# Cross-attention, MLP and normalised cross-attention on one core: the norm weights folded into the next matrices, three-product values and projection, the last two inverse head norms on VectorE

## The reference

```python
# layer 0 (a and b in the kernel)
q = layernorm(x, ln1_w, ln1_b) @ Wq            # 16 heads of 16
k, v = split(layernorm(ctx, ln2_w, ln2_b) @ Wkv)
x = x + softmax(q k^T / 4) v @ Wproj + bproj
x = x + gelu(layernorm(x, ln3_w, ln3_b) @ W1 + b1) @ W2 + b2
# layer 1 (c in the kernel)
q = rotate(rmsnorm(x) * norm_w @ wq);  k, v = split(ctx @ wkv);  k = rotate(k)
q, k = q / |q|, k / |k|                        # per head
x = x + softmax(4 q k^T) v @ wout
```

## Time and profile before

| | us |
|---|---|
| median of 3 runs | 366.83 |
| the three runs | 367.35, 366.83, 364.96 |
| the profiled execution, whole | 367.27 |
| its span, first to last instruction | 365.5 |
| PE busy in the span | 357.3 (98%) |
| DVE, ACT, POOL busy | 279.1, 252.7, 193.5 |

### The profile page before, as it was taken

One profiled execution on the slowest core, in us unless ns is written; L12 is line 12 of the kernel. 1 busy time (PEld: TensorE's weight loads), 2 busy tenths in 40 slices (PEclk: granted clock), 3 DMA queues, 4 the chain that ended last, 5 costly groups with the idle time before them and its releaser, 6 DMA issues.

```text
span 365.5 us, 11432 instructions
## 1 busy us (share of the span) xinstructions
PE 357.3 (98%) x4510; PEld 324.4 (89%) x4510; DVE 279.1 (76%) x654; ACT 252.7 (69%) x490; POOL 193.5 (53%) x194
## 2 busy tenths in 40 slices
PE   8999999999999998999999999999999999999996
PEld 5988888898878887899999999999999999998885
DVE  3699989869598777767886777788877776868752
ACT  2267676676677575774578978976987779966662
POOL 2266433534835338304576458458466755477920
PEclk9999999999999999999999999999999999999999
DMA  7854001100000000000000000000200010000001
GB/s 180 220 178 143 29 28 53 28 27 27 4 3 2 24 2 2 8 6 13 3 11 13 13 2 3 22 27 3 70 13 13 5 37 27 16 28 16 17 16 43
DMA packets 15724, 12.55 MB, mean 34 GB/s; under 512 B 3252, under 2 KB 15032, under 8 KB 15672
## 3 DMA queue, kind: packets, MB, share of 16 engines
q1 hardware_dynamic: 15664, 11.83, 11.3%
q10 hardware_dynamic: 8, 0.00, 0.0%
HBM read 9.73 MB, written 2.10 MB: 32 GB/s over the span
## 4 chain that ended last, share of the span: by engine, by line
PE 90%; DVE 6%; issue 2%; ACT 1%; POOL 0%; DVEq 0%; POOLq 0%; ACTq 0%
PE banks_s L1166 12%; PE bank_qk L1046 10%; PE banks_s L1091 7%; PE bank_o L1178 7%; PE bank_y L1178 6%; PE bank_y L1230 4%; PE banks_s L1219 4%; PE bank_t L1126 4%; PE bank_qk L1068 3%; PE bank_y L1147 3%; PE bank_t L1046 3%; PE bank_qk L1072 3%; PE bank_o L1082 3%; DVE row_max L2153 3%; PE bank_o L1210 2%
## 5 line engine op out<-in xcount | busy, mean ns | idle before, releaser
L400 POOL TENSOR_TENSOR norm_inv<-norm_sq_min,minus_half 128x32 f32<-128x32 f32 x16 | 87.6, 5478 | 47.9 <-DVE norm_sq_min L2248 47.9
L354 POOL TENSOR_TENSOR masked<-qkT_r,halves_t 128x512 fp32r<-128x512 f32 x32 | 32.6, 1039 | 60.8 <-DVE qkT_r L2146 60.7
L2153 DVE TENSOR_REDUCE row_max<-banks_s 128x8 f32<-128x1024 f32 x32 | 37.6, 1216 | 2.9 <-PE banks_s L1091 2.5
L575 ACT ACTIVATE PT<-banks_s 128x1024 f32<-128x1024 f32 x32 | 31.1, 1022 | 10.0 <-PE banks_s L1115 9.7
L1166 PE MATMUL banks_s<-lnT_hi,W_hi 128*128 128x256 f32 x120 | 35.4, 295 | 0.0
L676 ACT ACTIVATE PT<-banks_s 128x1024 f32<-128x1024 f32 x32 | 31.5, 1024 | 5.5 <-PE banks_s L1219 5.2
L1166 PE MATMUL banks_s<-lnT_hi,W_lo 128*128 128x256 f32 x120 | 33.9, 282 | 0.0
L1166 PE MATMUL banks_s<-lnT_lo,W_hi 128*128 128x256 f32 x120 | 33.9, 282 | 0.0
L1091 PE MATMUL banks_s<-masked,qkT_r 32*128 32x256 f32 x768 | 31.5, 294 | 0.9 <-DVE row_max L2153 0.7
L1091 PEld LDWEIGHTS banks_s<-masked,qkT_r 32*128 32x128 f32 x768 | 25.0, 183 | 7.5 <-issue 4.7
L619 ACT ACTIVATE W_s<-banks_s,b_cols 128x256 f32<-128x256 f32 x60 | 25.0, 471 | 6.6 <-PE bank_y L1178 4.7
(11 more groups left out here) (180 smaller groups left out, 1084.8 us busy)
## 6 DMA issues: line engine op xcount, KB each, us to landing
x_all<-in_x SPq DMA_DIRECT2D x16, 128.0 KB, 2.1
W_s<-in_L_xattn_W SPq DMA_DIRECT2D x2, 1024.0 KB, 8.1
out<-x_all SPq DMA_DIRECT2D x16, 128.0 KB, 1.8
ctx_in<-in_ctx SPq DMA_DIRECT2D x16, 96.0 KB, 2.2
ctx_in<-in_ctx_T SPq DMA_DIRECT2D x16, 64.0 KB, 1.9
ctx_in<-in_ctx_T SPq DMA_DIRECT2D x16, 32.0 KB, 2.1
Wq_s<-in_L_xattn_Wq SPq DMA_DIRECT2D x1, 256.0 KB, 3.6
Wkv_s<-in_L_xattn_Wkv SPq DMA_DIRECT2D x1, 256.0 KB, 3.7
```

What stands on the lines that cost most here:

```text
L354: nc.gpsimd.tensor_tensor(masked[:, r, 1, :, half, :], qkT_r[:, r, 1, :, :].bitcast(fp32), ones, ALU.mult)\
L400: nc.gpsimd.tensor_tensor(norm_inv[:, j, :], norm_sq_min[:, j, :], minus_half[:, :], ALU.pow).then_inc(c_norm_inv, 1)
L575: nc.scalar.activation(PT[:, 2 * h:2 * h + 2, :], banks_s[:, 2 * h:2 * h + 2, :], ACT.Exp, scale=HD ** -0.5)\
L2153: v.tensor_reduce(row_max[:, 8 * h:8 * h + 8], banks_s[:, 2 * h:2 * h + 2, :].rearrange("p n (r k) -> p (n r) k", k=TOK), AX.X, ALU.max).t ...
```

## The change

- ln1's and ln2's weights are multiplied into Wq and Wkv (`query_weight`, `keys_weight`, `values_weight_hi`, `values_weight_lo`), ln1's bias becomes `q_bias`, added in the evacuation, ln2's bias an extra row of the context matrix against a column of ones in `yn`. ln3's weight is multiplied into W1 in `w1_split`, its bias goes into `b1_all`. `centre` and `scale` become one `normalise` (for b: `normalise_b`), a `tensor_scalar`.
- The row spreading and 26 transposes at the start go; `query_bias_mm` (8 records), `context_bias_mm` (4 records, 512 wide) and `mlp_bias_mm` (16 matmuls one column wide, 32 records) come.
- `values_a` and `project_a` are three-product (`split_mm`). GpSimd's `values_in` and VectorE's `on_lo_a` make the low parts.
- For tiles 14 and 15, `head_norms_root` on VectorE (10 dependent operations on 128x32) takes the place of GpSimd's power.
- All lists are reordered, SyncE's loads of c and stores too. PE's `busy` transposes after the first 14 are 110 where they were 98: 7, 9, 8, 8 up to the first `shifted_a`, then 4, 4, 9 among the last tiles of a, 6 in b, and 3, 4, 7, 12, 8, 3, 8, 10 in the last tiles of c (before: 4, 7, 10; 6, 8; 6, 10, 5, 9, 4, 11, 8, 10).

```diff
-WARM_EARLY, WARM_LATE = 14, 26
+WARM = 14
+            def values_in(t):
+                j = t % 2
+                pool.wait_ge(A["inT_ready"], t + 1)
+                wait(pool, A["v_mm"], t - 1)
+                nc.gpsimd.tensor_copy(v_in[:, j, 0, :, :], inT[:, j, 2:4, :]).then_inc(a_v_in_hi, 1)
+                pool.wait_ge(a_v_in_hi, t + 1)
+                nc.gpsimd.tensor_tensor(v_in[:, j, 1, :, :], inT[:, j, 2:4, :], v_in[:, j, 0, :, :].bitcast(fp32), ALU.subtract).then_inc(a_v_in_lo, 1)
...
-                act.dma_start(row_1[:, C1 * n:C1 * n + C1], v.unsqueeze(0)).then_inc(ln_rows_loaded, LOADED)
+            act.dma_start(ln_cols[:, 0, :], ln1_w.rearrange("(t p) -> p t", p=128), allow_slow_non_contiguous=True).then_inc(ln_rows_loaded, LOADED)
...
+            act.wait_ge(bias_zeroed, 1)
+            act.dma_start(bias_2[:, 0, C2B:C2B + 1], ln2_b[0:128].unsqueeze(1), allow_slow_non_contiguous=True).then_inc(ln_rows_loaded, LOADED)
...
-                nc.scalar.activation(qkT_r[:, t % RING, 0, :, :], bank_qk[:, :].rearrange("p (a b) -> p a b", a=4), ACT.Copy)\
-                    .then_inc(a_qk_hi, 1)
+                for m in range(KT):
+                    nc.scalar.activation(qkT_r[:, r, 0, m, :], bank_qk[:, TOK * m:TOK * m + TOK], ACT.Identity, bias=q_bias[:, m:m + 1])\
+                        .then_inc(a_q_hi, 1)
+                nc.scalar.activation(qkT_r[:, r, 0, KT:, :], by_row(bank_qk[:, 2 * TOK:]), ACT.Copy).then_inc(a_k_hi, 1)
...
-                    last = mm(bank_o[:, 0:C1], inT[:, t % 2, 2 + k, :], Wkv_s[:, k, C1:], start=k == 0, stop=k == 1)
-                last.then_inc(A["v_mm"], 1)
+                pe.wait_ge(a_v_in_lo, t + 1)
+                split_mm(bank_o[:, 0:C1], v_in[:, t % 2, :, :, :], wkv_r[:, :, :, C1:]).then_inc(A["v_mm"], 1)
...
+                pe.wait_ge(a_onT_lo, t + 1)
+                split_mm(bank_y[:, 0:C1], onT_r[:, :, :, :], wout_r[:, :, :, :]).then_inc(A["proj_mm"], 1)
+            def mlp_bias_mm():
+                pe.wait_ge(w1_loaded, LOADED)
+                pe.wait_ge(w_b1_loaded, 4 * LOADED)
+                for m in range(HM):
+                    for k in range(KT):
+                        last = mm(bank_y[:, m:m + 1], W1_s[:, k, 128 * m:128 * m + 128], ln3_cols[:, 1, k:k + 1], start=k == 0, stop=k == KT - 1)
+                last.then_inc(b1_mm, 1)
...
-            pe.wait_ge(ln_rows_loaded, 4 * LOADED)
-            pe.wait_ge(ones_ready, 1)
-            mm(bank_qk[:, :], one_row, row_1, start=True, stop=True)
-            mm(bank_o[:, 0:2 * C2], one_row, row_2, start=True, stop=True).then_inc(rows_spread, 1)
-            for n in range(WARM_LATE):
-                nc.tensor.transpose(bank_s[n % 4][:, 0:128], ident[:, :], ident[:, :])
+            pe.wait_ge(ln_rows_loaded, 6 * LOADED)
             pe.wait_ge(bank_zeroed, 1)
-            busy(4, bank_t)
+            busy(7, bank_t)
+            query_bias_mm()
             inputs_a(0)
-            busy(7, bank_o)
+            context_bias_mm()
+            busy(9, bank_y)
+            pe.wait_ge(q_bias_ready, 1)
             queries_keys_a(0)
...
+            def normalise(t):
...
+                v.tensor_scalar(xn[:, j, :], tile_of(t), mean_var[:, j, 0:1], rstd[:, j, 0:1], ALU.subtract, ALU.mult).then_inc(A["norm_done"], 1)
+                v.tensor_scalar(yn[:, j, 0:C2], ctx_in[:, t % AHEAD, 0:C2], mean_var[:, j, 2:3], rstd[:, j, 1:2], ALU.subtract, ALU.mult)\
+                    .then_inc(A["norm_done"], 1)
...
+            def head_norms_root(t):
...
+                v.tensor_scalar(root.bitcast(int32), norm.bitcast(int32), -0.5, HALF_EXPONENT, ALU.mult, ALU.add).then_inc(c_root, 1)
+                for n in range(3):
+                    dve.wait_ge(c_root, done + 3 * n + 1)
+                    v.tensor_tensor(root_sq[:, :], root, root, ALU.mult).then_inc(c_root, 1)
+                    dve.wait_ge(c_root, done + 3 * n + 2)
+                    v.scalar_tensor_tensor(root_sq[:, :], root_sq[:, :], -0.5, norm, ALU.mult, ALU.mult).then_inc(c_root, 1)
+                    dve.wait_ge(c_root, done + 3 * n + 3)
+                    v.scalar_tensor_tensor(root, root_sq[:, :], 1.5, root, ALU.add, ALU.mult).then_inc(c_root if n < 2 else c_norm_root, 1)
```

More of the change, by code:

```diff
@@ new lines, in queries_keys_lo @@
+                dve.wait_ge(a_k_hi, t + 1)
+                for m in range(KT):
+                    last = v.scalar_tensor_tensor(qkT_r[:, r, 1, m, :], bank_qk[:, TOK * m:TOK * m + TOK], q_bias[:, m:m + 1],
+                                                  qkT_r[:, r, 0, m, :].bitcast(fp32), ALU.add, ALU.subtract)
+                last.then_inc(a_q_lo, 1)
+                v.tensor_tensor(qkT_r[:, r, 1, KT:, :], by_row(bank_qk[:, 2 * TOK:]), qkT_r[:, r, 0, KT:, :].bitcast(fp32),
+                                ALU.subtract).then_inc(a_k_lo, 1)
@@ L2357, in _ @@
+            maxima_split(6)
+            on_lo_a(3)
+            w1_split(1)
+            residual_a(3)
+            heads_a(4)
+            on_lo_a(4)
+            statistics(11)
+            statistics(12)
+            queries_keys_lo(8)
+            normalise(11)
+            residual_a(4)
+            maxima(7)
             heads_a(5)
-            queries_keys_lo(8)
-            maxima(7)
             maxima_split(7)
-            residual_a(4)
             queries_keys_lo(9)
             maxima(8)
-            residual_a(5)
@@ L2469, in _ @@
             turned(2)
+            res_b(2, 0)
+            stats_b(4)
             square_sums(2)
-            units(1)
-            res_b(2, 0)
+            units_lo(1)
+            turns(3)
+            split_lnT(3)
+            turned(3)
+            out_weight()
             res_b(2, 1)
-            units_lo(1)
             units(2)
-            split_lnT(3)
+            square_sums(3)
             heads_c(0)
-            turns(3)
+            split_hT(3, 0)
             units_lo(2)
-            turned(3)
@@ L2495, in _ @@
-            inputs_lo(5)
             res_b(3, 0)
-            centre_b(4)
+            units_lo(3)
+            stats_b(5)
             res_b(3, 1)
-            scale_b(4)
-            units_lo(3)
+            split_lnT(4)
             units(4)
-            residual_c(1)
-            split_lnT(4)
             heads_c(2)
-            units_lo(4)
             turns(5)
             turned(5)
+            units_lo(4)
+            out_lo(2)
+            heads_c(3)
+            square_sums(5)
+            inputs_lo(6)
@@ L2508, in _ @@
             split_hT(4, 0)
-            square_sums(5)
-            out_lo(2)
-            stats_b(5)
             residual_c(2)
-            inputs_lo(6)
-            heads_c(3)
-            centre_b(5)
+            out_lo(3)
             split_hT(4, 1)
             split_hT(4, 2)
-            out_lo(3)
             turns(6)
+            turned(6)
             split_hT(4, 3)
+            square_sums(6)
+            normalise_b(5)
+            res_b(4, 0)
             inputs_lo(7)
-            turned(6)
@@ L2523, in _ @@
             units(5)
[L2524 to L2528 removed]
             res_b(4, 1)
             stats_b(6)
+            units_lo(5)
+            residual_c(3)
+            units(6)
             split_lnT(5)
[L2532 removed]
+            normalise_b(6)
             heads_c(4)
+            units_lo(6)
             turns(7)
[L2535 to L2537 removed]
             turned(7)
+            split_hT(5, 0)
```

1495 lines of the change are left out of this document (780 added, 715 removed).

## The result

The changed kernel takes 375.74 us (median of 4 runs, 375.03 to 377.66), the kernel before 366.44, measured beside it; the ratio is 1.026, 95% interval 1.023 to 1.030. It is 9.3 us slower, where 1.4 us less was forecast, and lies outside the range of 361.0 to 370.0. The profiled execution took 377.66 us (span 375.9), 10.4 more span than before.

What follows compares the result with a forecast made beforehand. PE (TensorE) was taken as the bound from its first product to c's last tiles. Terms -0.7 +0.7 -4.5 +2.9 +0 +0.2 = -1.4 from 366.83 gave 365.4 us; own range 363.5 to 367.5, overall 361.0 to 370.0.

Steps and rivals of the forecast that it cites:

- Start: Up to `shifted_a(0)`: spreading and transposes go, a wait for column loads comes; `shifted_a(0)` 0.7 us earlier.
- Late columns: Rival at the start: column loads land 7.6 us after the last issue, +3.9, 369.3 us; chance 0.08.
- Values of tile 2: In a's list: values of tile 2 now come behind `shifted_a(0)`, 0.7 us more.
- Three products: Values and projection of a: three fp32r products save 0.155 us in each of 29 groups, 4.5 us less.
- One-column products: `mlp_bias_mm` in a's list: 32 records of 0.111 us replace six transposes, 2.9 us more.
- cheap bias products: Rival: the 32 bias records take 0.035 us each and half of PE's waits goes, 361.6 us; chance 0.28.
- Work beside PE: VectorE, ScalarE and GpSimd work, loads, stores and idle transposes stay hidden behind PE: zero.
- The shared way: Rival in a: more GpSimd operations reading SBUF delay VectorE's `max_cols` operations and PE, 371.1 us; chance 0.15.
- Tail: Last tiles of c: VectorE roots replace GpSimd's powers, but `scores_c(14)` stands behind `units_T(15)`; 0.2 us more.
- a tail that gains: Rival in the last tiles: dependent small operations take 0.10 us instead of 0.20, 363.4 us; chance 0.12.

Runs made afterwards that it cites:

- e8: e7 with GpSimd's powers for tiles 14 and 15 and the last tiles' order of the kernel before: 365.30 us, 0.997 of before.
- e1: Changed kernel without the 32 one-column MLP bias products (third norm's bias left out): 371.25 us, 1.010 of before.
- e7: e1 with 16 more transposes before the wait for the columns and 3 instead of 7 behind it: 366.24 us, 1.000 of before.
- e2: Changed kernel with 32 transposes of 128 columns in place of the one-column bias products (third norm's bias left out): 374.08 us, 1.019 of before.
- e5: Changed kernel with its 32 one-column records in four parts of 8, other TensorE work between them: 375.79 us, 1.022 of before.
- e9: e8 with a's values and projection in two fp32 products per group instead of three fp32r: 369.00 us, 1.008 of before.
- e12: e11 with the same bias products on 48 moving columns instead of one: 367.50 us, 1.003 of before.
- e11: Changed kernel, everything computed, one-column products kept, with the start and tail of e8: 369.48 us, 1.010 of before.
- e10: e8 with the third norm's weight and bias applied by VectorE as in the kernel before, no bias products: 369.34 us, 1.008 of before.
- e15: e12 with its 48-column products in three parts, less 23 idle transposes outside the start and last tiles: 365.53 us, 0.997 of before.
- e16: e15 also without the nine and eight idle transposes of the start: 365.62 us, 0.998 of before.
- e17: Kernel before with 26 transposes ahead of the two spreading products and 14 behind, instead of 14 and 26: 364.90 us, 0.997 of before.
- e6: Kernel before with 64 records of unused one-column products in place of six transposes behind tile 1's maxima: 379.24 us, 1.034 of before.

## Why the prediction was wrong

The steps, in the order of the sum. The ladder that the profiled executions give, in spans: e8 363.3, start +6.1 (`shifted_a(0)` at 32.58 for 26.50), products' length +2.2, 6.8 us at half rate behind them +3.4, tail +0.9, together 375.9, as measured. In medians, e8 365.3 with a start of +5.0 (e1 less e7) gives 376.8 against 375.7, because the starts are mixed.

Against the kernel before, forecast -1.4 and +10.4 in the profiled executions differ by 11.8. The misses below add up to it: start 4.4, clock 3.4, three products 2.9, tail 0.7, values of tile 2 0.1, an open 0.9, and 0.7 less for the products' length.

- **Start, forecast -0.7.** This is the step that failed first: "Behind the landing PE has 7 transposes (1.5), 8 bias records (1.2), ... 7.1 in all", with a first product at 14.1. The landing was nearly right (7.5 for 7), but the first product stood at 17.33. Of the 9.8 us between, the four records 512 wide took 3.85 where I had put 2.6, the nine transposes 1.97 for 1.0, and the eight bias records 1.56 for 1.2: I had priced the last of them at full rate. From the first product to `shifted_a(0)` it took 15.25 us, where 14.1 us was forecast (the first queries at half rate, and 1.3 us of waiting for the maxima). In e1's profiled execution the product stood at 14.11, 6.8 behind the landing; that one execution meets the forecast is luck. What failed is that I took the slow rate of the old start as a property of the stage that ends near 13.7, and saw the removal of the two spreading products only as work gone. The new wait leaves a gap of 2.6 to 3.3 us; behind it a rate that was already full fell again in e1, e2 and e5, and the lasting full rate came between 12 and 19 us. With the gap filled (e7) it never fell. `shifted_a(0)` 3.7 later, where 0.7 earlier was forecast. Late columns, the rival for this place, didn't happen.
- **Values of tile 2, +0.7.** 0.85.
- **Three products, -4.5.** The right direction, mis-sized: 0.055 a group and not 0.155, 1.6 us in 30 groups. The error is 0.71 "of the chain": one group between others of its kind. The earlier trace rows already showed 0.81 behind fp32 work; the honest unit was the mean from start to next start over all groups in their lists, 0.90 before against the 0.80 that L1046 had in c. A count of borders hides where they stand: in the new lists an fp32 group would hold 0.93 and slow its neighbours, so there three products are worth 3.7 (e9), and the new lists have taken most of the difference.
- **One-column products, +2.9.** Their record is 0.112 for 0.111, and 2.2 us reach the end (e12 less e8). The rival "cheap bias products" is refuted by the record. Not foreseen, and put at nothing: that they lower the clock behind them, 3.4 us in the changed kernel. This is the second step that failed. The Trainium skill (TensorE: Matmul & The Clock Gate, LDWEIGHTS), cited for the price, agrees with the trace: 0.107 estimated, 0.112 measured. The Trainium skill (TensorE: Matmul & The Clock Gate, HAM oscillation) names stretches without work as what lowers the clock; here it fell while TensorE was busy 2.00 of 2.00 us, so here the measurement decides, and e12 against e11 shows that the one moving column is what matters.
- **Work beside PE, 0.** Idle time of TensorE from 20 to 150 us is 4.0 us for 3.1. The transposes, priced at zero, gave 0.4 when taken out. What I called "VectorE saves time in a stage that PE fills: zero" is too easy a phrase: with the old norm put back, 4.0 us are lost in these lists (e10). A full stage says that VectorE is in time now, not by how much.
- **The shared way.** It didn't come where it was feared: operations that write `max_cols` and take over 0.6 us were 7 in the trace before and are 5 after. `normalise` met it, as the prediction said it would: 7 of its 32 operations take 0.78 to 1.14 us with a GpSimd operation beside them, where they take 0.37 and 0.41 alone (not "at most 0.35"). That is some 4 us of VectorE's time, and TensorE's idle time rose by 0.9 in all.
- **Tail, +0.2.** 0.9 (e7 less e8). The root's steps start 0.23 apart, 2.2 for the 2.0 put; `units(15)` comes at 357.7 and `scores_c(15)` at 364.3, 26.5 us behind the last down_b; before it was 25.6. Counted from the last down_b, `units(15)` is 1.0 earlier than before where 1.3 was forecast, and `units_T(15)`, which stands between `units_lo(14)` and `scores_c(14)` on TensorE and had no price, takes another 0.5. Direction and mechanism as told (`scores_c(14)` behind `units_T(15)`), the size too small; "a tail that gains" is refuted.

What stays open: why the same code gets its lasting full rate at 12 us in one execution and at 19 in another, and 0.9 us of the stretch behind `shifted_a(0)` (+6.6 measured, of which products 2.2, clock 3.4, tail 0.9, values of tile 2 0.85 and three products -1.6 make 5.7), which lies among the new lists' waits and transposes. From `shifted_a(0)` on, idle transposes hold 1.15 us more in e8 than in the kernel before and waits 0.6 more, other work 0.9 less; taking 23 transposes out gave back 0.4 (e15).

Of the versions that compute everything the best are 0.3% under the kernel before and 2.7 to 2.9% under the changed one: e15 (365.5; e16 is the same within the noise) has all of the change but the Newton tail, with wide bias products in parts and a filled start, and e17 (364.9) is the kernel before with its start's transposes moved. With an early full rate in both, the change is not faster than the kernel before: 365.5 against 364.9, not measured side by side.

## What to carry to other kernels

A product with one moving column costs the time of its weights and, in a run of them, the clock behind it; with the column broadcast (to 48 columns in e12) only the time was left. Read TensorE's clock column, and the durations of a known form beside it, in every stage that becomes "full", above all in the first 20 us: here a wait put into the start moved the lasting full rate from 7 us (e7) to 12 (e1) or 19 (changed kernel), and filling the wait with transposes brought it back. Price a kind of work by the mean from start to next start over all its places in the list, not by its best neighbour.

## What the runs showed of the hardware that was not expected

- One-column fp32 products (32 records in 3.7 us) were followed by 3.4 (e11) to 6.8 us (changed kernel) at half the granted clock, and by some 10 us in two of e11's six executions; 64 records brought 13.6 us (e6). The same 32 records with 48 columns (e12), or 32 transposes (e2), brought none.
- A gap of 2.6 to 3.3 us, from 4.8 us on, was followed by a fall from the full rate at 8 to 9 us in e1, e2 and e5; in e7, without the gap, there was no fall.
- Where the full rate came early and stayed, the executions of a kernel lie within 0.2 to 0.4% (e8: 364.9 to 365.5; e17: 364.1 to 365.4); where the start left it to chance, within 1.2% (e1: 368.0 to 372.4).
- The granted clock column can read 1.00 up to 19 us while the records take twice their usual time (L1139 x8: 1.91 us at 17.33, 1.06 in e7).
